# Order of VectorE's work in the expert stage, deeper routing, attention's first loads a stage earlier, and the result written from the last stage

## What is computed

```
x = x + 0.5 * moe_ffn(layernorm(x))       # 4 experts, W1: 256 x 1024 each, one shared Wo: 1024 x 256
x = x + causal_softmax_attention(layernorm(x))           # 16 heads of 16
x = x + 0.5 * moe_ffn(layernorm(x))       # the same weights once more
x = x + 0.5 * fp4_ffn(layernorm(x))       # 704 wide; weights and activations quantised to 4 bits
x = x + causal_linear_attention(layernorm(x))
x = x + 0.5 * fp4_ffn(layernorm(x))

moe_ffn(x):  e = argmax(x @ W_router)     # one expert for a token
             y = gelu(x @ W1[e] + b1[e]) @ Wo + bo + x
             return layernorm(y) * gamma + beta
```

## Time and profile before

| what | us |
|---|---|
| median of 3 runs (lowest, highest) | 2456.76 (2456.46, 2456.95) |
| profiled execution, its time | 2456.01 |
| profiled execution, its span | 2454.3 |
| TensorE busy with matmuls | 2098.6 |
| VectorE busy | 1456.1 |
| ScalarE busy | 1022.0 |
| GpSimd busy | 934.0 |

### The profile page before, as it was taken

One profiled execution on the slowest core, in us unless ns is written; L12 is line 12 of the kernel. 1 busy time (PEld: TensorE's weight loads), 2 busy tenths in 40 slices (PEclk: granted clock), 3 DMA queues, 4 the chain that ended last, 5 costly groups with the idle time before them and its releaser, 6 DMA issues. The chain is left out here.

```text
span 2454.3 us, 42217 instructions
## 1 busy us (share of the span) xinstructions
PE 2098.6 (86%) x13729; PEld 1456.6 (59%) x13729; DVE 1456.1 (59%) x4048; ACT 1022.0 (42%) x2367; POOL 934.0 (38%) x1160
## 2 busy tenths in 40 slices
PE   7599994969999999894566798599997999879996
PEld 6499992524444444474555697366665666556674
DVE  4222235678888888253333322799966766488883
ACT  3233332416666666541111232233334666533431
POOL 5322227511111121151111133666645666455552
PEclk9999997969999999986787899799998999989998
DMA  4355553454433331113222354200000000000002
GB/s 153 111 194 194 194 170 96 155 99 56 59 53 53 53 53 27 37 61 124 95 93 93 106 202 136 62 13 17 4 1 1 2 2 2 2 1 0 0 1 69
DMA packets 101903, 174.51 MB, mean 71 GB/s; under 512 B 14768, under 2 KB 66256, under 8 KB 101712
## 3 DMA queue, kind: packets, MB, share of 16 engines
q1 hardware_dynamic: 95184, 154.27, 23.5%
q0 software_dynamic: 6528, 17.83, 2.3%
HBM read 136.01 MB, written 35.78 MB: 70 GB/s over the span
## 5 line engine op out<-in xcount | busy, mean ns | idle before, releaser
L1083 DVE TENSOR_REDUCE a_part_max<-a_psS 128x1 f32<-128x512 f32 (+3 forms) x608 | 362.4, 654 | 76.6 <-PE a_psS L1011 68.1
L1139 ACT ACTIVATE a_PT<-a_psE 128x512 f32<-128x512 f32 (+1 forms) x608 | 309.1, 584 | 189.2 <-PE a_psE L1025 172.3
L570 PE MATMUL e_psH<-e_xsT,e_w 128*128 128x128 f32 x2240 | 291.5, 294 | 0.0
L570 PEld LDWEIGHTS e_psH<-e_xsT,e_w 128*128 128x128 f32 x2240 | 287.6, 211 | 0.1
L621 DVE TENSOR_TENSOR e_y<-e_psY,e_xr 128x256 f32<-128x256 f32 x70 | 29.7, 425 | 409.6 <-PE e_psY L579 405.4
L1005 PE MATMUL a_psS<-a_sk,a_sq 96*128 96x512 bf16 (+3 forms) x768 | 234.0, 341 | 23.7 <-DMA a_sk<-qk_parts 19.8
L579 PE MATMUL e_psY<-wo_moe,e_gT 128*128 128x256 f32 x1120 | 253.0, 379 | 0.0
L644 POOL TENSOR_TENSOR e_rstd<-e_moments,minus_half 128x1 f32<-128x1 f32 x70 | 45.1, 645 | 543.3 <-DVE e_moments L122 543.3
L986 POOL TENSOR_SCALAR_AFFINE_SELECT a_PT<-a_PT 128x512 f32<-128x512 f32 x128 | 81.2, 635 | 419.3 <-ACT a_PT L1139 419.3
L601 ACT ACTIVATE e_gT<-e_psH,e_bias 128x128 f32<-128x128 f32 x560 | 159.4, 368 | 163.5 <-PE e_psH L570 161.9
L1025 PE MATMUL a_psE<-a_sq,a_sk 98*128 98x512 bf16 (+3 forms) x768 | 224.3, 329 | 2.5 <-ACT a_PT L1139 1.4
(11 more groups left out here) (283 smaller groups left out, 3946.2 us busy)
## 6 DMA issues: line engine op xcount, KB each, us to landing
e_w<-w_in SPq DMA_DIRECT2D x70, 1024.0 KB, 5.0
a_sq<-qk_parts SPq DMA_DIRECT2D x96, 128.0 KB, 4.5
a_sk<-qk_parts SPq DMA_DIRECT2D x96, 128.0 KB, 7.5
e_xs<-sorted_x SPq DMA_DIRECT2D x70, 128.0 KB, 2.0
e_xr<-sorted_x SPq DMA_DIRECT2D x70, 128.0 KB, 4.2
sorted_y<-e_yo SPq DMA_DIRECT2D x70, 128.0 KB
X<-x_in SPq DMA_DIRECT2D x8, 512.0 KB, 6.4
qk_parts<-q_hi SPq DMA_DIRECT2D x32, 128.0 KB, 1.7
```

What stands on the lines that cost most here:

```text
L570: mm = pe.matmul(psH[p][:, n * P:(n + 1) * P], w1[p][:, k, n * P:(n + 1) * P], xsT[p][:, k, :], start=k == 0, stop=k == KD - 1)
L1083: dve.tensor_reduce(part_max[:, c, h0:h0 + heads, qt], psS[place % RING][:, 0:heads * n].rearrange("p (h k) -> p h k", h=heads), AX.X, ALU ...
L1139: act.activation(PT[kt % 2][:, h0:h0 + heads, q0:q0 + n], psE[e % RING][:, 0:heads * n].rearrange("p (h q) -> p h q", h=heads), ACT.Exp, s ...
```

## The change

Four parts of the kernel are changed.

- **Expert stages.** In VectorE's step, `quantize_weights` moves to the head of the list. The first expert stage, which quantises nothing, gets the three memsets of `sk`'s spare rows, one in each of three steps.
- **Routing.** The moments go in groups of four tiles instead of two. `measure`, `norm`, `evacuate`, `turn` and `router` stand further apart (the numbers in the lists), ScalarE's norm is for one tile a step, TensorE's order in a step is turn, count, router, and GpSimd scatters one tile a step. One-hots, the triangle and the ones of the count are bf16. The rows of zeros stand ahead of each expert's region and are written once by a plain DMA in `r0_`, so the four scatters of zeros at the end are gone. The table is computed by 21 instructions over wider tensors instead of 25 and 2. The setup has four more GpSimd operations and three more casts.
- **Attention's first stacks.** `sq` and `sk` are allocated ahead of the first expert stage. SP issues iteration 0's 12 loads in the qkv stage, two behind the stores of each of the last six groups, and attention's `load(0)` is gone.
- **The result.** The second fp4 feed-forward writes `out` in eight pieces of four tiles as they are done; `finish_phase` is gone.

```diff
@@ route_phase, VectorE
-            moment_chain = Chain(dve, moment, MOMENTS, st.pause[:], tiles=2)
+            moment_chain = Chain(dve, moment, MOMENTS, st.pause[:])
...
             pipeline(dve, TILES, ([(2, join)] if after_attention else []) +
-                     [(J, measure, 2), (J + 2, take_shift, 2), (J + 8, choose, 4), (J + 10, put, 4)], unroll=4, loop=False)
+                     [(J + 12, put, 4), (J, measure, 4), (J + 2, take_shift, 4), (J + 10, choose, 4)], unroll=4, loop=False)
@@ J is the lag behind the joins of the second routing stage
-    J = 3 if after_attention else 0
+    J = 5 if after_attention else 0
@@ ScalarE
-                     [(J + 3, evacuate), (J + 2, norm, 2)], unroll=4, loop=False)
+                     [(J + 5, evacuate), (J + 4, norm)], unroll=4, loop=False)
@@ GpSimd
-            pipeline(pool, TILES, [(J, root, 2), (J + 10, scatter, 4)], unroll=4, loop=False)
-
-            pool.wait_ge(padded, 2)
-            for e in range(EXPERTS):
-                pool.indirect_dma_start(st.sorted_x[:, :], bass.IndirectOffsetOnAxis(ap=pad_slot[:, e:e + 1], axis=0),
-                                        st.zeros[:], None).then_inc(scattered, 16)
-            pool.wait_ge(scattered, 16 * (TILES + EXPERTS))
+            pipeline(pool, TILES, [(J, root, 4), (J + 12, scatter)], unroll=4, loop=False)
+            pool.wait_ge(scattered, 16 * TILES)
@@ TensorE
-                     [(J + 9, count_up, 4), (J + 4, router), (J + 3, turn)], unroll=4, loop=False)
-
-            pe.wait_ge(placed, PLACED * NG)
-            pe.matmul(psN[:, GE:GE + EXPERTS], st.ones[:], before[NG % 2][:], start=True, stop=True).then_inc(counted, 1)
+                     [(J + 5, turn), (J + 11, count_up, 4), (J + 6, router)], unroll=4, loop=False)
+
+            if after_attention:
+                pe.wait_ge(joined, TILES)
+            pe.matmul(psA[0][:, 0:EXPERTS], st.ones[:], before[NG % 2][:], start=True, stop=True).then_inc(counted, 1)
@@ expert_phase, VectorE
+            def set_spare_rows(t, p):
+
+                if t < len(st.sk):
+                    dve.memset(st.sk[t][SROWS:P, :, :], 1.0)
+
+            pipeline(dve, SLOTS, [(0, quantize_weights)] * (fp4 is not None) + [(0, take_bias), (2, finish), (3, norm)] +
+                     [(3, set_spare_rows)] * (fp4 is None), loop=False)
@@ qkv_phase, SP
+            def load_stacks(g, p):
+
+                if g >= FIRST_BATCH:
+                    if g == FIRST_BATCH:
+                        for s in stored:
+                            sp.wait_ge(s, 48 * FIRST_BATCH)
+                    load_block(sp, st, 0, g - FIRST_BATCH)
+
+            pipeline(sp, NG, [(0, store), (0, load_stacks)], loop=False)
@@ attention_phase
-            load(0)
             load(1)
             maxima(0)
@@ fp4_ffn_phase, SP, in the second of its two runs
+                rows = result.rearrange("(t p) d -> p t d", p=P)
+                for t in range(0, TILES, OUT_TILES):
+                    sp.wait_ge(added, t + OUT_TILES)
+                    sp.dma_start(rows[:, t:t + OUT_TILES, :], st.X[:, t:t + OUT_TILES, :]).then_inc(written, 16)
+                sp.wait_ge(written, 16 * (TILES // OUT_TILES))
```

More of the change, by code:

```diff
@@ L352, in _ @@
-            for e in range(1, EXPERTS):
-                ins = dve.tensor_scalar(beyond[:, e - 1, :], place[:], float(e * REGION), skip[:, e - 1:e],
-                                        ALU.is_ge, ALU.mult)
-                (q.link if e == EXPERTS - 1 else q.done)(ins)
-            for e in range(1, EXPERTS):
-                q.link(dve.tensor_tensor(place[:], place[:], beyond[:, e - 1, :], ALU.subtract))
+            q.done(dve.scalar_tensor_tensor(out=place_step[:, 0:EXPERTS], in0=tiles_of[:], scalar=float(P), in1=count,
+                                            op0=ALU.mult, op1=ALU.subtract))
@@ new lines, in _ @@
+            q.done(dve.tensor_scalar(slot_step[:, EXPERTS:], count, -1.0, float(REGION), ALU.mult, ALU.add))
+            q.link(dve.tensor_tensor_scan(first[:], st.ones[:, 0:EXPERTS], tiles_of[:], 0.0, ALU.mult, ALU.add))
+            q.done(dve.tensor_scalar(slot_at[:, 0:EXPERTS], first[:], -1.0, None, ALU.add))
+            q.done(dve.tensor_copy(slot_at[:, EXPERTS:], first[:]))
+            q.link(dve.tensor_scalar(slot_step[:, 0:EXPERTS], place_step[:, 0:EXPERTS], -1.0, None, ALU.mult))
+            q.link(dve.tensor_tensor(slot_after[:], each(st.slot_f[:], SLOTS), over(slot_at[:], SLOTS), ALU.is_ge))
@@ new lines, in _ @@
+            q.done(dve.tensor_copy(place_at[:, EXPERTS:], st.next_f[:]))
+            q.done(dve.scalar_tensor_tensor(out=place_at[:, 0:EXPERTS], in0=tiles_of[:], scalar=float(P), in1=st.last_f[:],
+                                            op0=ALU.mult, op1=ALU.add))
+            q.link(dve.tensor_scalar(place_step[:, EXPERTS:], slot_step[:, EXPERTS:], -1.0, None, ALU.mult))
+            dve.wait_ge(placed, PLACED * NG)
+            q.link(dve.tensor_tensor(place_after[:], each(place[:], TILES), over(place_at[:], TILES), ALU.is_ge))
@@ L1075, in _ @@
             dve.memset(max_bf[:, 2:4, :], 0.0).then_inc(padded, 1)
-            for i in range(3):
-                dve.memset(sk[i][SROWS:P, :, :], 1.0).then_inc(padded, 1)
             def reduce(it, u):
@@ L2002, in build @@
         run(linear_attention_phase, "l_")
[L2003 to L2017 removed]
+        run(fp4_ffn_phase, "f1_", False, out)
 def kernel(**inputs):
```

232 lines of the change are left out of this document (118 added, 114 removed).

## The result

The changed kernel takes 2268.49 us (median of 4 runs, 2266.27 to 2270.61), against 2456.61 before: a ratio of 0.9235, with a 95% interval of 0.9219 to 0.9251. The forecast was 2278 us, with a range of 2262 to 2303. Its profiled execution took 2266.27 us, with a span of 2264.6, so 189.7 us less than the span before.

What follows compares the result with a forecast made beforehand. It looked first at the second expert stage's ring (finish, quantise, turn, up, down), where TensorE waits for VectorE's quantising. 2456.0 - 130 - 18.4 - 7 - 11.5 - 11 = 2278.1, stated as 2278 us, range 2262 to 2303.

Steps and rivals of the forecast that it cites:

- Second experts: Second expert stage: quantising ahead of finish takes 16 rounds from 249.1 to 124.3 us and removes the first stall: -130.
- The rival in which it binds from a ring of 9 us: Second expert stage: VectorE's round stretches from 6.4 to about 9 us, TensorE waits 1.2 us a round: 2298 us; chance 0.15.
- First routing: First routing stage: a group falls from 9.25 to 7.4 us and four padding scatters go: -18.4 us.
- six passes, 1.2 us: First routing stage: with bf16 one-hots and masks the count-up needs six passes, 1.2 us, instead of ten, 2.0 us.
- Second routing: Second routing stage: shorter count-ups and no padding let the last scatter end at 1107.5 instead of 1114.4: -7 us.
- The deeper pipeline: Second routing stage: two steps more and groups of four delay the last scatters; at the bound it eats the whole gain.
- Attention's stacks: Attention's start: ten of twelve loads land in the qkv stage, so the first score matmul starts at about 505.9: -11.5 us.
- The result: Kernel's end: only the last 512 KB remain to move after the last add, ending at 2443.3: -11 us.
- The rival that the first routing stage rises to the upper clock: First routing stage: shorter waits raise TensorE's clock, a tile takes 1.35 us, GpSimd's 6.3 us bind: 2270 us; chance 0.18.
- The clock of the second experts: Second expert stage: rival that TensorE doesn't get its upper clock back, rounds of 12 us: 2346 us; chance 0.03.
- Slower: Qkv stage: stores held until a pair lands cost 29.7 us per group, eating the 178 us gain; chance 0.03.
- the held stores in the qkv stage: Qkv stage: each of six groups pays a pair's landing, 4 to 10 us: 2302 to 2338 us; chance 0.05.

Runs made afterwards that it cites:

- experiment 1: Changed kernel with quantising put back behind finish and norm in VectorE's step: 2408.28 us, second expert stage 411.6 us.
- experiment 2: Kernel before with one edit, quantising at the head of VectorE's step in the second expert stage: 2323.19 us, ratio 0.9461.
- experiment 3: Changed kernel with six extra 128x256 adds behind each quantised piece on VectorE: second expert stage 282.6 us, a round 7.91 us.
- later: The unedited changed kernel, profiled twice again beside the experiments: 2277.05 us and 2274.47 us.
- experiment 4: Changed kernel with router one step earlier in both routing stages: first routing stage 85.0 us against 75.4, second 110.4 against 98.1.
- experiment 7: Changed kernel with the count's one-hots, triangle and ones in fp32 again: routing stages 85.0 and 104.5 us, +9.6 and +6.4.
- experiment 6: Changed kernel with the rows of zeros written by four scatters again in both routing stages: 80.75 and 103.48 us, +5.4 in each.
- experiment 11: Changed kernel with ScalarE's norm ahead of its take-out in routing and the result in pieces of two tiles: 2270.25 us, ratio 0.9242.
- experiment 10: Changed kernel with the result written as one 4.2 MB piece: 15.3 us from the last add's start to the end, against 4.3.
- experiment 8: Changed kernel with choose, count_up, put and scatter one step earlier in routing: first routing stage 77.9 us, second 102.7.
- experiment 9: Changed kernel with attention's first twelve loads back at its head, out of the qkv stage: 2290.86 us, attention 517.65 us.
- the last control: The unedited changed kernel measured again in the last set of experiments: 2274.47 us, ratio 0.9262.

## Why the prediction was right, point by point

1. **Second experts, -130 forecast, -133.5 measured.** The mechanism is shown both ways (experiments 1 and 2). A round was put at 7.77 us and is 7.51: the piece's two transposes cost 0.12 us beyond the 7.39, not their whole 0.38, which is the length of their row with its tail; the next matmul starts 0.22 behind the first of them. (The 15.57 us of a round before are a mean with a last, short one of 9.6, from 1385.14 to 1394.72; the fifteen ahead of it take 15.97 each. The sum is the same.) What VectorE has to do was put at 6.4 us; it is 7.50 - 1.09 = 6.4 with the register read and 5.9 when VectorE is late (experiment 3). The rival in which it binds from a ring of 9 us is not ruled out by the mechanism, only by 1.6 us of room.
2. **First routing, -18.4 forecast, -23.5 measured (-21.4 and -21.9 later).** The order argument held: 1.6 us a tile forecast, 1.65 measured, and experiment 4 gives 2.02 without it. The mis-sized term is the count-up: "six passes, 1.2 us", measured 0.58, because the bf16 matmuls cost 0.16 us together (experiment 7). The group takes 6.85 us instead of 7.4, which is 3.3 us over the six groups of the sum. A second error ran the other way: the first scatter starts at 24.8, not 22.4. A third term was not in the sum: in the middle of the stage a group's scatters start 3.2 us behind its slots (28.54 to 31.72), because the root of a later group stands ahead of them on GpSimd; the last three groups have no root ahead, and the last one starts 0.3 us behind its slots (67.69 to 67.96). So it starts at 68.0, where the sum had 73. The padding is worth 5.4 us in each stage (experiment 6), forecast 5.0.
3. **Second routing, -7 forecast, -9.0 measured, and -3.5 and -4.0 later.** The forecast lies between, and that is in part luck, since the stage changes by 5 us from profile to profile. In the first profile the last 16 scatters are back to back, as forecast, from 66.5 us behind the stage's start instead of 68.5; in the later two they begin at 69 and stand still once for 2.5 us. The padding and the count-up give together more than the forecast (5.4 and 6.4 us by experiments 6 and 7), so something takes back a part. The deeper pipeline was supposed to; that is argued and was not measured by itself.
4. **Attention's stacks, -11.5 forecast, -10.1 measured.** The first score matmul starts 2.3 us behind the stage's start, as forecast, 11.4 us less than before. 1.3 us are given back behind it. In the first iteration TensorE now waits 1.76 us for the transfer of the row maxima (the row at 511.77), against 0.19 before. That explains only a part: in the profile of experiment 11, whose attention is the same, the wait is 0.18 us, and the stage still takes 504.5 us, 10.7 less than before. The rest stays open. It is within the term's bounds.
5. **The result, -11 forecast, -13.1 measured.** 11.5 us of it come behind the last add: 4.3 us instead of 15.8, where the forecast's terms give 4.8. Of these terms the 1 us of latency and the 1.5 of transfer stand in no row by themselves; the profile has 2.9 us from the issue of such a piece to its landing (median of 8). The other 1.6 us are a delay that the profile before has and most others haven't (experiment 10), so without luck the term is 11.5.

The rival that the first routing stage rises to the upper clock did not come about, although TensorE is now busy for 47.89 of 74.0 us there and waits shorter: the transposes stay at 0.67 to 0.69 us, even in experiment 11, at 1.17 us a tile. By the Trainium skill ("TensorE: Matmul & The Clock Gate", Part 1) sustained activity would release the clock; no profile here shows it in this stage. The clock of the second experts did rise, to 1.00. Slower, and the held stores in the qkv stage, did not appear: 125.0 us against 124.9.

## What to carry to other kernels

Where two engines pass work to each other once a round, look at what the receiving engine's list does first: a job that does not need this round's result belongs ahead of the one that waits for it. One list entry was worth 132 us here. The same question, asked of ScalarE's norm and take-out, gave 4 us more. Before a change of type is sized by passes, look for a row with the shape and type: with 4 to 16 columns fp32 cost ten times bf16. And keep a profile of the changed kernel without edits beside each set of experiments, since differences of 5 us in a stage come without any edit.

## What was not expected of the hardware

**The clock rises at different times in the same code.** In the second routing stage the turning of attention's result (L428) goes 3.0, 2.8, 1.82 us from tile to tile in ten profiles of fourteen, in nearly the same way in an eleventh, and in the other three (experiments 8, 9 and 10) 3.0 five times before it falls to 1.82. The matmul's own row tells the level; the tenth experiment:

```profile
990.87 0.63 PE L428 MATMUL r_psY<-ident,V 128*128 128x128 f32 x2
...
999.79 0.63 PE L428 MATMUL r_psY<-ident,V 128*128 128x128 f32 x2
```

and the changed kernel that ran beside it, the third and the fourth tile:

```profile
992.35 0.38 PE L428 MATMUL r_psY<-ident,V 128*128 128x128 f32 x2
...
994.17 0.38 PE L428 MATMUL r_psY<-ident,V 128*128 128x128 f32 x2
```

This costs 4.3 us (the first tile of routing is turned 24.9 instead of 20.6 us behind the stage's start) and has nothing to do with the edits: those of experiments 9 and 10 lie in other stages, and that of experiment 8 moves only steps that come later. 0.63 is the lower of the two levels (1.2 GHz), 0.38 the upper (2.4 GHz).

**A hand-over of 0.4 us that sometimes takes 1.2.** The rest of what the later profiles lose in the second routing stage comes once a group. In the first profile VectorE's `put` (L326) starts 0.4 us behind the last matmul of the count; in the last control it is

```profile
1034.30 0.37 PE L471 MATMUL r_psN<-r_before,ones 128*128 128x16 f32 x2
...
1035.51 0.17 DVE L326 TENSOR_TENSOR r_rank<-r_psN,region_f 128x16 f32<-128x16 f32 x1 [1.13 <-PE r_psN L471]
...
1035.91 0.38 PE L428 MATMUL r_psY<-ident,V 128*128 128x128 f32 x2
1037.06 0.38 ACT L398 ACTIVATE r_yT<-r_psY 128x256 f32<-128x256 f32 x1 [1.74 <-PE r_psY L428]
```

1.2 us for VectorE, and 1.15 instead of 0.42 for ScalarE, so that a group takes 8.4 us instead of 7.6. In the first routing stage ScalarE and VectorE are both held in this way once, near 61 us. Both later profiles of the changed kernel show both, the first shows neither. What holds back TensorE's signal stays open; no experiment was made on it.
